# Neighbour rows by shifted copies, biases by broadcast loads, all orders redrawn

## Time and profile before

| | us |
|---|---|
| median of 3 runs | 1048.71 (1045.53 to 1049.8) |
| the profiled execution | 1047.97 |
| its span, first to last instruction | 1045.9 |
| PE busy (share of the span) | 949.0 (91%) |
| PE weight loads | 797.0 (76%) |
| DVE busy | 813.9 (78%) |
| POOL busy | 534.5 (51%) |
| ACT busy | 379.4 (36%) |
| DMA moved | 99.73 MB, mean 95 GB/s |

### The profile page before, as it was taken

One profiled execution on the slowest core, in us unless ns is written; L12 is line 12 of the kernel. 1 busy time (PEld: TensorE's weight loads), 2 busy tenths in 40 slices (PEclk: granted clock), 3 DMA queues, 4 the chain that ended last, 5 costly groups with the idle time before them and its releaser, 6 DMA issues.

```text
span 1045.9 us, 18382 instructions
## 1 busy us (share of the span) xinstructions
PE 949.0 (91%) x6188; PEld 797.0 (76%) x6248; DVE 813.9 (78%) x1377; ACT 379.4 (36%) x698; POOL 534.5 (51%) x731
## 2 busy tenths in 40 slices
PE   2469899999999999999999999999999999998985
PEld 1248697887879797887879797887969788796862
DVE  6668779697887969687887969788796968777663
ACT  3344333434343333425333243434333342523221
POOL 2543538373654639274554738365463827454331
PEclk9669999999999999999999999999999999999996
DMA  7435131333234232223323232322424133310000
GB/s 228 162 122 191 53 120 61 116 107 102 81 91 132 70 114 80 101 97 100 107 88 116 64 119 101 102 81 91 132 71 131 62 103 112 100 42 21 1 21 20
DMA packets 67170, 99.73 MB, mean 95 GB/s; under 512 B 6345, under 2 KB 23251, under 8 KB 67077
## 3 DMA queue, kind: packets, MB, share of 16 engines
q1 hardware_dynamic: 62676, 92.38, 27.8%
q10 hardware_dynamic: 4400, 6.18, 1.8%
HBM read 90.15 MB, written 8.39 MB: 94 GB/s over the span
## 4 chain that ended last, share of the span: by engine, by line
PE 51%; DVE 32%; issue 8%; POOL 5%; ACT 2%; DMA 1%; DVEq 0%; SPq 0%; ACTq 0%; POOLq 0%
PE bank L1260 28%; PE bank L1252 12%; DVE work L1020 6%; PE bank L1395 5%; POOL work L419 4%; DVE w_r L828 3%; PE bank L1245 3%; DVE work L1029 3%; DVE work L1074 2%; DVE work L983 2%; DVE amath L997 2%; DVE work L947 2%; PE bank L1307 2%; PE bank L1403 1%; DVE work L941 1%
## 5 line engine op out<-in xcount | busy, mean ns | idle before, releaser
L419 POOL TENSOR_TENSOR work<-work 128x448 f32<-128x448 f32 (+3 forms) x224 | 190.1, 849 | 30.7 <-DVE work L1020 11.7
L1260 PE MATMUL bank<-x2h,wg_r 128*128 128x256 f32 x1536 | 187.7, 278 | 0.0
L1260 PEld LDWEIGHTS bank<-x2h,wg_r 128*128 128x128 f32 x1536 | 182.7, 188 | 1.7 <-issue 0.5
L1020 DVE TENSOR_TENSOR work<-bank,work 128x512 f32<-128x512 f32 (+7 forms) x256 | 105.6, 448 | 17.1 <-POOL work L419 15.7
L1395 PE MATMUL bank<-gh,amath 128*128 128x512 f32 x384 | 101.0, 405 | 17.9 <-DVE amath L997 11.7
L435 POOL TENSOR_TENSOR work<-work 128x512 f32<-128x512 f32 x32 | 54.6, 1707 | 122.0 <-DMA work<-in_L_cond_beta 121.9
L1252 PE MATMUL bank<-w_r,xh 128*128 128x512 f32 x384 | 112.1, 430 | 3.2 <-DVE w_r L828 3.2
L427 POOL TENSOR_TENSOR work<-work,scal 128x1 f32<-128x1 f32 x64 | 18.0, 282 | 185.7 <-DVE work L935 138.7
L828 DVE TENSOR_TENSOR w_r<-w_land,w_r 128x1024 fp32r<-128x1024 f32 x64 | 90.5, 1414 | 20.6 <-ACT w_r L563 20.6
L1395 PEld LDWEIGHTS bank<-gh,amath 128*128 128x128 f32 x384 | 68.4, 188 | 48.8 <-DVE amath L997 26.3
L1260 PE MATMUL bank<-x2h,wsoma_r 128*128 128x256 f32 x768 | 103.6, 285 | 0.4 <-ACT work L625 0.4
(11 more groups left out here) (164 smaller groups left out, 1632.6 us busy)
## 6 DMA issues: line engine op xcount, KB each, us to landing
w_land<-in_L_cond_weight SPq DMA_DIRECT2D x64, 512.0 KB, 3.7
w_t<-in_L_cond_W SPq DMA_DIRECT2D x64, 256.0 KB, 3.1
work<-in_xT SPq DMA_DIRECT2D x32, 256.0 KB, 4.0
work<-in_x SPq DMA_DIRECT2D x32, 256.0 KB, 3.8
work<-in_L_cond_beta SPq DMA_DIRECT2D x32, 256.0 KB, 3.8
gamma_t<-in_L_cond_gamma SPq DMA_DIRECT2D x32, 256.0 KB, 4.1
out<-work SPq DMA_DIRECT2D x32, 256.0 KB, 2.1
work<-in_L_cond_Wg ACTq DMA_DIRECT2D x2, 1024.0 KB, 7.0
```

Of the source, the lines that this page charges most:

```text
L419: g_.tensor_tensor(dst, dst, src, ALU.add).then_inc(S["acc_ready"], 1)
L1020: ins = v_.tensor_tensor(dst, src, g_q[:, 2 * half:2 * half + 2, :, 0:width], ALU.mult)
L1260: ins = mm(dst, weight[:, w_part, first_block + a, o * P:(o + 1) * P], act[:, x_part, a], start=(not onto and a + w_part + x_part == 0), s ...
```

## The change

The last block no longer uses TensorE. SP copies x3 inside SBUF, shifted by one row down into `before` and one row up into `after`, with the border rows taken from inside (four DMAs a sample). POOL adds the two (`row_neighbours`). ACT forms `slope = -zR*x3 + (1 + zR - 2zX - 2zY)` into `after`, POOL multiplies it by x3 (`quadratic`), and DVE adds the two neighbour sums with their factors. The square, the `mix` matrices and the row factors go.

Biases b0 and b2 of a sample are loaded as broadcast rows of 256 KB into one shared buffer and added by POOL: b0 to x before `x1_row`, x1 to b2 before `y_row`. b1 is loaded as a column and is the bias operand of the relu. The three matmuls, tables, one-hots and their rows go. `mod_scaled` and `mod_on_lo_rows` move from DVE to ACT; the high parts of vj are made by ACT straight from `blend_n`, the low parts by DVE. `lap_factors` moves from the start to step 0. The order of calls is new on every engine, setup calls included, and the cut between steps lies elsewhere. The new DVE order has, at a step, out_centred of sample 1 of the pair before, then final_sum and final of sample 0, then x3_row of sample 1. The core of the diff, with the new orders of SP and POOL (removed lines of the orders left out):

```diff
+        before, after = buf("before"), buf("after")
+        slope, fin = after, nb
...
-        STEPS = range(-3, NP + 2)
+        STEPS = range(-5, NP + 1)
...
+                def load_b0(p, r):
+                    b = 2 * p + r
+                    if b:
+                        sp.wait_ge(S["y_ready"], b)
+                    sp.dma_start(b0_t[:, :], l0_b[subject_of(b)].rearrange("l c -> (l c)").partition_broadcast(P)).then_inc(S["b0_loaded"], 16)
+
+                def load_b1(p, r):
+                    b = 2 * p + r
+                    if b:
+                        sp.wait_ge(S["h_ready"], b)
+                    sp.dma_start(b1_t[:, r:r + 1], l1_b1[language_of(b)].rearrange("l (h a) -> (l h) a", a=1)).then_inc(S["b1_loaded"], 16)
+
+                def load_b2(p, r):
+                    b = 2 * p + r
+                    sp.wait_ge(S["xb0_ready"], b + 1)
+                    sp.dma_start(b2_t[:, :], l1_b2[language_of(b)].rearrange("l c -> (l c)").partition_broadcast(P)).then_inc(S["b2_loaded"], 16)
...
+                def shift_rows(p, r):
+                    b = 2 * p + r
+                    sp.wait_ge(S["x3_ready"], b + 1)
+                    if b:
+                        sp.wait_ge(S["lap_ready"], b)
+                        sp.wait_ge(S["fin_ready"], b)
+                    for dst, src in ((before[1:P], x3[0:P - 1]), (before[0:1], x3[1:2]), (after[0:P - 1], x3[1:P]), (after[P - 1:P], x3[P - 2:P - 1])):
+                        sp.dma_start(dst, src).then_inc(S["shifted"], 16)
...
+                        load_x(i + 2, 1)
+                        load_w1(i + 2, 1)
+                        load_w0(i + 2, 1, 1)
+                        load_gamma(i + 2, 0)
+                        load_b1(i + 2, 1)
+                    if live(i - 1):
+                        shift_rows(i - 1, 1)
                     if live(i + 2):
+                        load_b0(i + 2, 1)
+                    if live(i + 3):
+                        load_xT(i + 3, 0)
+                        load_w0(i + 3, 0, 0)
+                    if live(i + 2):
+                        load_b2(i + 2, 1)
+                        load_beta(i + 2, 1)
+                        load_w2(i + 2, 1)
+                        load_gamma(i + 2, 1)
                     if live(i - 1):
+                        store(i - 1, 1)
                     if live(i + 3):
+                        load_w1(i + 3, 0)
+                        load_w0(i + 3, 0, 1)
+                    if live(i):
+                        shift_rows(i, 0)
+                    if live(i + 3):
+                        load_b0(i + 3, 0)
+                        load_x(i + 3, 0)
+                        load_w2(i + 3, 0)
+                        load_beta(i + 3, 0)
+                        load_w0(i + 3, 1, 0)
+                    if live(i):
+                        store(i, 0)
+                    if live(i + 3):
+                        load_xT(i + 3, 1)
+                        load_b1(i + 3, 0)
+                        load_b2(i + 3, 0)
                 sp.wait_ge(S["out_stored"], 16 * NB)
...
-            def vj_lo_parts():
-                for j in range(Q):
-                    pool.wait_ge(vj_hi, j + 1)
-                    g_.tensor_tensor(vj[P // 2:P, j], vtmp[P // 2:P, j % 2], vj[P // 2:P, j].bitcast(f32), ALU.subtract).then_inc(vj_lo, 1)
...
+            def x_plus_b0(p, r):
+                b = 2 * p + r
+                pool.wait_ge(S["b0_loaded"], 16 * (b + 1))
+                pool.wait_ge(S[f"x_loaded_{r}"], 16 * (p + 1))
+                g_.tensor_tensor(xs[:, r], xs[:, r], b0_t[:, :], ALU.add).then_inc(S["xb0_ready"], 1)
+
+            def x1_plus_b2(p, r):
+                b = 2 * p + r
+                pool.wait_ge(S["b2_loaded"], 16 * (b + 1))
+                pool.wait_ge(S["x1_ready"], b + 1)
+                g_.tensor_tensor(b2_t[:, :], b2_t[:, :], xs[:, r], ALU.add).then_inc(S["xb2_ready"], 1)
...
+            def row_neighbours(p, r):
+                b = 2 * p + r
+                pool.wait_ge(S["shifted"], 4 * 16 * (b + 1))
+                g_.tensor_tensor(before, before, after, ALU.add).then_inc(S["rows_ready"], 1)
+
+            def quadratic(p, r):
+                b = 2 * p + r
+                pool.wait_ge(S["slope_ready"], b + 1)
+                g_.tensor_tensor(after, slope, x3, ALU.mult).then_inc(S["quad_ready"], 1)
...
+                if live(i + 2):
+                    x1_plus_b2(i + 2, 0)
+                if i == -2:
+                    mask_spread()
+                if live(i + 2):
+                    x_lo(i + 2, 1)
                 if live(i - 1):
                     neighbours(i - 1, 1)
+                    row_neighbours(i - 1, 1)
                 if live(i + 2):
                     rstd(mv_a, rs_a, 1, i + 2, 0)
+                if live(i - 1):
+                    quadratic(i - 1, 1)
+                if live(i + 2):
+                    x_plus_b0(i + 2, 1)
+                    x1_plus_b2(i + 2, 1)
                     x_plus_beta(i + 2, 1)
+                if live(i + 3):
+                    x_lo(i + 3, 0)
                 if live(i + 1):
                     add_terms(i + 1, 2)
                     add_terms(i + 1, 3)
                     add_terms(i + 1, 4)
                     add_terms(i + 1, 5)
+                if live(i):
+                    rstd(mv_c, rs_c, 2, i, 0)
+                if live(i + 1):
                     add_terms(i + 1, 6)
                     add_terms(i + 1, 7)
+                    add_terms(i + 1, 8)
+                if live(i):
+                    neighbours(i, 0)
+                if i == -2:
+                    pool.wait_ge(const_loaded, N_CONST * 16)
+                if live(i + 2):
+                    x2_plus_beta(i + 2, 0)
+                    rstd(mv_a, rs_a, 1, i + 2, 1)
+                if live(i + 1):
+                    add_terms(i + 1, 9)
+                if live(i):
+                    row_neighbours(i, 0)
+                    quadratic(i, 0)
+                if live(i + 3):
+                    x_plus_b0(i + 3, 0)
+                if live(i):
+                    rstd(mv_c, rs_c, 2, i, 1)
+                if live(i + 3):
+                    x_plus_beta(i + 3, 0)
+                if live(i + 2):
+                    x2_plus_beta(i + 2, 1)
...
-                a_.activation(hT, hT_ps, ACT.Relu).then_inc(S["h_ready"], 1)
+                act.wait_ge(S["b1_loaded"], 16 * (b + 1))
+                a_.activation(hT, hT_ps, ACT.Relu, bias=b1_t[:, r:r + 1]).then_inc(S["h_ready"], 1)
...
+            def mod_scaled(p):
+                act.wait_ge(S["mt_ready"], p + 1)
+                a_.activation(m_q, m_q, ACT.Copy, scale=0.25, bias=0.5).then_inc(S["m_ready"], 1)
+
+            def mod_on_lo_rows(p):
+                act.wait_ge(S["m_ready"], p + 1)
+                if past(p, 1):
+                    act.wait_ge(S["state_done"], NG * 2 * p)
+                a_.activation(msh, m_q, ACT.Copy, scale=lo_rows[:, :]).then_inc(S["msh_ready"], 1)
...
-            def square(p, r):
-                b = 2 * p + r
-                act.wait_ge(S["lap_done"], b + 1)
-                act.wait_ge(S["nb_ready"], b + 1)
-                act.wait_ge(S["nbe_ready"], b + 1)
-                a_.activation(sq, x3, ACT.Square).then_inc(S["sq_ready"], 1)
+            def slopes(p, r):
+                b = 2 * p + r
+                act.wait_ge(S["x3_ready"], b + 1)
+                act.wait_ge(S["rows_ready"], b + 1)
+                a_.activation(slope, x3, ACT.Identity, scale=zt[:, b, 3:4], bias=zt[:, b, 0:1]).then_inc(S["slope_ready"], 1)
...
             def vj_hi_parts(distances):
+                act.wait_ge(blend_copied, 1)
                 for j in distances:
-                    act.wait_ge(vj_full, j + 1)
-                    a_.activation(vj[:, j], vtmp[:, j % 2], ACT.Copy).then_inc(vj_hi, 1)
+                    a_.activation(vj[:, j], blend_n[:, :], ACT.Copy, scale=alpha_j[:, j:j + 1]).then_inc(vj_hi, 1)
...
-            def vj_parts(distances):
+            def vj_lo_parts(distances):
+                lows = slice(P // 2, P)
                 for j in distances:
-                    if j >= 2:
-                        dve.wait_ge(vj_lo, j - 1)
-                    v_.tensor_scalar(vtmp[:, j % 2], blend_n[:, :], alpha_j[:, j:j + 1], None, ALU.mult).then_inc(vj_full, 1)
+                    dve.wait_ge(vj_hi, j + 1)
+                    v_.scalar_tensor_tensor(vj[lows, j], blend_n[lows, :], alpha_j[lows, j:j + 1], vj[lows, j].bitcast(f32),
+                                            ALU.mult, ALU.subtract).then_inc(vj_lo, 1)
...
-                dve.wait_ge(S[f"x_loaded_{r}"], 16 * (p + 1))
+                dve.wait_ge(S["xb0_ready"], b + 1)
...
+                dve.wait_ge(S["xb2_ready"], b + 1)
-                v_.tensor_tensor(xs[:, r], B_A2[:, :], xs[:, r], ALU.add).then_inc(S["y_ready"], 1)
+                v_.tensor_tensor(xs[:, r], B_A2[:, :], b2_t[:, :], ALU.add).then_inc(S["y_ready"], 1)
...
```

(61 more changed lines are left out.)

610 lines of the change are left out of this document (217 added, 393 removed).

## The result

The changed kernel took 1584.12 us, the median of four runs (1577.32 to 1589.91); the kernel before took 1047.12 beside it. The ratio is 1.5107 (95% interval 1.5063 to 1.5151): 51% slower, where 1013.6 us had been forecast and 990 to 1044 allowed.

What follows compares the result with a forecast made beforehand. TensorE was taken as the bound, DVE second at 82%. Start 107.0, 13 periods of 57.7, pairs 14 and 15 at 55.9 and 50.8, drain 46.7, factors 1.0: span 1011.5, plus 2.1 is 1013.6 us; range 990 to 1044.

Steps and rivals of the forecast that it cites:

- DMA and SP: Loads and row copies on SP's queue: SP has room, copies land in 2.1 to 4.1 us, cost taken as 0.
- I count some 34 MB on 100: no bandwidth matter: DMA traffic: the added bias loads and SBUF copies, some 34 MB on 100, would not matter for bandwidth.
- Rival D: SP's queue: the row shift at its head brings x and w0 late, 1 us a sample, 1044 us; chance 0.07.
- Rival C: DVE and POOL: their turns become the bound, at 90% filled a period of 60.9 us, 1061 us; chance 0.13.
- TensorE loses 2.7 us a period: TensorE in the steady pairs: laplacian 1.8 and bias matmuls 0.9 us go, 57.6 to 54.9 us a period.
- 0.8 us comes back in waits: Steady period: DVE and POOL's crowding returns 0.8 us as TensorE waits, bounds 0 and +4; new period 57.7 us.
- DVE and POOL's busy time: Steady period: DVE below 51 us and POOL 37 to 40 us a period.
- The two signs of the turns: DVE and POOL in turn: L828 slower in the mean than 1.41 us, and add_terms slower.
- Setup -12: Before pair 0: earlier w0_lo, shorter vj path and moved factors save 12 us, bounds 3 and 22; states at 107.
- The factors' 1 us: First steady period: the laplacian's factors, moved out of the setup, reappear there and add 1 us.
- Drain +4.5: End of the run: x3 to quadratic takes 7.0 us, the drain costs 4.5 us more (1 to 8), 46.7 us.

Runs made afterwards that it cites:

- E5: E1 plus two 127-row copies a sample from a constant tile to scratch HBM, behind the shift, that no engine computes on: 1516.32 us, ratio 1.4489.
- E8: E1 with each of POOL's additions x+b0 and x1+b2 replaced by two zero fills of a 128x512 tile: 1021.62 us, ratio 0.974.
- E1: The changed kernel with each 127-row copy cut into 112 and 15 rows, six DMAs a sample instead of four: 1044.62 us, ratio 0.9988.
- E3: E1 with each shift cut into 113 and 14 rows instead of 112 and 15: 1526.9 us, ratio 1.459.
- E4: E1 with each shift cut into 96 and 31 rows instead of 112 and 15: 1104.94 us, ratio 1.0558.
- E7: E1 with POOL's row neighbours and quadratic done on one column of 512: 1009.9 us, ratio 0.9618.
- V1: The kernel before with only the setup's new vj, high parts by ACT straight from blend_n, low parts by DVE: 1041.97 us, ratio 0.9927.

## Why the prediction was wrong

**The step that failed** is one sentence of "DMA and SP": "The row copies are timed on a store, the shortest to land in the page, 2.1 us, and at most 4.1 like a broadcast load." All rows it leaned on are transfers of 128 rows. The copy of 127 rows looks like them in bytes (254 KB, 256 KB), but its landing is not theirs: 24.9 us for the four together. The upper bound was no bound, since none of those rows has the new operation's row count. "I count some 34 MB on 100: no bandwidth matter" was right in bytes (133.26 MB against 99.73) and no help: what ran out was one engine's rate. The sum had 3.5 us for the four issues and the landing together; the issues alone took 14.7.

**Rival D** named the place and the mechanism, loads behind the shift at the head of SP's queue, and E5 showed that slow copies there are worth 45% even where nothing computes on them. It was priced at 1 us a sample from the same 2.1 us, and given 0.07. Rival C looked for a slower kernel in the turns of DVE and POOL; this kernel is not slow by them, but the mechanism is real: E8 prices two of the four additions at 1.0 us a period.

**The other steps**, which E1 lets one read, in the prediction's own terms: the second sample's states of pairs 0, 13, 14 and 15 start at 115.83, 881.27, 938.97 and 990.00 us, the end is at 1041.5; in the kernel before 119.00, 893.66, 951.49, 1003.68 and 1045.9. With the copies mended the forecast of 1013.6 would still have missed 1044.62 by 31 us, and the range ends at 1044:
- *TensorE loses 2.7 us a period.* The matmuls are gone, but busy time fell by 1.7, from 57.6 to 55.9: gate, soma and state passes lasted longer. A third of the gain was never there, and its cause is open.
- *0.8 us comes back in waits.* It was 1.1: the waits grew from 2.0 to 3.1 us a period, so 0.6 of the 2.7 are left. The period is 58.88 us over all thirteen, against 59.59, where 57.7 was forecast. E8 shows that turns at SBUF with two of the four additions cost 1.0 us of it; without their reads the forecast would nearly have held, 57.87. The 0.8 was a sum of small waits, and did not count that DVE itself becomes longer.
- *DVE and POOL's busy time* came out as forecast, 49.5 and 38.3 us a period, under 51 and within 37 to 40. The two signs of the turns split: add_terms became slower (849 to 892 ns in the mean), the w0 split did not (1414 to 1366). A busy share that comes out right says nothing of the order in which the turns fall.
- *Setup -12.* It was -3.2 in E1, at the very bound of 3. One trace is not exact here: in the six whose setup is the same (the changed kernel, E1, E3, E4, E5, E7) these states start between 113.0 and 119.7 us. In the chain of waits of E1's setup the vj parts still stand on the way, now DVE's, 9.2 us where 5.6 were priced and 3 of them were to come due, and loads before them:

```profile
34.73 4.99 DMA w_land<-in_L_cond_weight
...
57.83 4.37 DMA work<-in_x
...
64.41 5.36 DVE vj L897 x4
70.16 3.79 DVE vj L897 x4
```

  In V1 the same edit gave 4.7 us, where 9.4 had been taken. Taking one link out of a setup lets the next load stand in its place, and each load has its own time. The factors' 1 us does not show: the first period of E1 is 57.3 us, shorter than the others.
- *Drain +4.5.* It was +9.3 (51.5 against 42.2 us), outside 1 to 8. x3 to quadratic's end takes 8.8 us a sample in E1 (x3 ends at 1016.83, L455 at 1025.65) and not 7.0, with two issues more; that is twice 1.8 of the missing 4.8 us, and 1.1 lies ahead of the first x3.

The sum of these: -3.2 of setup, -9.2 over 13 periods, -1.3 for the two pairs that follow, +9.3 of drain, together -4.4 of span, which is E1's 1041.5 against 1045.9.

## What to carry to other kernels

Before a transfer is priced by a row of the trace, compare its slowest dimension with that row's: a copy shifted by one row has 127, a prime number, and goes over one of sixteen engines; cut it into 112 + 15. A slow transfer costs what stands behind it in its queue, read or not, so look there before counting bytes. Where two engines read SBUF in turn, busy time hides the price; fills of the same size in place of the reads show it. An edit that adds or drops even a small tensor moves what lies behind it, and a change of under 1% can be that and nothing else: put the bytes back as padding before crediting the edit.

## What the runs showed that was not expected

- 508 KB from SBUF to SBUF in two copies of 127 rows: 24.9 us, 21 GB/s, 25 GB/s in the drain; in 112 + 15 rows 5.4 us with six issues.
- SP is held by the issues of such copies: 14.7 us for four, 4.2 us for the six.
- 32 bytes of layout change the period by 0.47 us of 59.6 with the same instructions, through TensorE's gate pass (11.6 to 12.0 us) and temporal pass (6.1 to 6.3); in E1, where waits set the period, the same 32 bytes lengthen the passes by 0.5 us a period and the period by nothing.
- Two such copies a sample with nothing computing on them (E5): 87% of the loss, a 256 KB load behind them landing after 17.9 us instead of 3.5.
- Two POOL fills of 128x512 in place of each of two additions with reads a sample: 1021.6 us against 1044.6, though POOL is busy only 31 us less.
